# Moving two transposing chunks behind P @ V in an attention and feed-forward kernel

## The reference

```python
def reference(x, qkv_w, qkv_b, proj_w, proj_b, w_gate, w_up, w_down):
    xn = layernorm(x)                                  # x: 8 x 512 x 256
    q, k, v = split_heads(xn @ qkv_w + qkv_b)          # 16 heads of 16
    p = softmax(einsum('bnhd,bmhd->bhnm', q, k) * 0.25)
    attn = merge(einsum('bhnm,bmhd->bnhd', p, v)) @ proj_w + proj_b
    gate, up = xn @ (w_gate / 127).T, xn @ (w_up / 127).T   # hidden 768, integer weights
    ffn = (silu(gate) * up) @ (w_down / 127).T
    return x + attn + ffn
```

## Time and profile before

| | |
|---|---|
| three runs | 628.84, 630.44, 630.52 us (median 630.44) |
| profiled execution, its own time | 631.72 us |
| its span | 629.8 us, mean granted TensorE clock 0.997 |
| TensorE busy | 605.6 us (96%) |
| VectorE busy | 490.8 us (78%) |
| ScalarE busy | 373.6 us (59%) |
| GpSimd busy | 172.4 us (27%) |

### The profile page before, as it was taken

One profiled execution on the slowest core, in us unless ns is written; L12 is line 12 of the kernel. 1 busy time (PEld: TensorE's weight loads), 2 busy tenths in 40 slices (PEclk: granted clock), 3 DMA queues, 4 the chain that ended last, 5 costly groups with the idle time before them and its releaser, 6 DMA issues.

```text
span 629.8 us, 10979 instructions
## 1 busy us (share of the span) xinstructions
PE 605.6 (96%) x3616; PEld 329.5 (52%) x3616; DVE 490.8 (78%) x647; ACT 373.6 (59%) x483; POOL 172.4 (27%) x181
## 2 busy tenths in 40 slices
PE   7898999999999999999999999999999999999885
PEld 6654455554645555554545545455555455554434
DVE  5897887788887887888887887878878777878712
ACT  3545665666566565675566564766557655666571
POOL 3215144220621225220532215221252202222210
PEclk9999999999999999999999999999999999999998
DMA  8770181114612184203812166012822037221101
GB/s 277 230 120 3 68 234 52 53 36 163 157 36 50 59 245 82 51 4 130 202 50 51 34 180 162 12 50 93 230 64 51 3 124 180 51 51 36 35 2 36
DMA packets 38204, 58.98 MB, mean 94 GB/s; under 512 B 6048, under 2 KB 21280, under 8 KB 38176
## 3 DMA queue, kind: packets, MB, share of 16 engines
q1 hardware_dynamic: 38176, 58.61, 34.3%
HBM read 37.10 MB, written 20.97 MB: 92 GB/s over the span
## 4 chain that ended last, share of the span: by engine, by line
PE 85%; DVE 6%; ACT 4%; issue 3%; DMA 1%; POOL 1%; SPq 0%; ACTq 0%; DVEq 0%; POOLq 0%
PE dense L910 36%; PE o_bank L900 19%; PE st_bank L869 16%; PE s_bank L886 11%; DVE neg_max L681 3%; ACT probs L562 2%; DMA probs<-in_L_attn_qkv_w 1%; PE dense L924 1%; PE dense L941 1%; DVE o_blocks L742 1%; ACT qk_parts L578 1%; POOL xn L489 1%; PE s_bank L869 0%; PE dense L968 0%; DVE w_gl L733 0%
## 5 line engine op out<-in xcount | busy, mean ns | idle before, releaser
L562 ACT ACTIVATE probs<-st_bank 128x1024 f32<-128x1024 f32 x250 | 255.9, 1024 | 211.0 <-PE st_bank L869 206.7
L681 DVE TENSOR_REDUCE neg_max<-s_bank 128x2 f32<-128x1024 f32 x250 | 304.8, 1219 | 75.8 <-PE s_bank L886 75.0
L900 PE MATMUL o_bank<-probs,v_ones 128*32 128x512 f32 x1024 | 137.2, 608 | 3.8 <-ACT probs L562 3.8
L869 PE MATMUL st_bank<-q_stack,k_stack 50*128 50x512 f32 x500 | 124.7, 495 | 4.4 <-ACT probs L562 4.2
L497 POOL TENSOR_TENSOR hid_tl<-hid,hid_th 128x512 fp32r<-128x512 f32 x48 | 61.7, 1285 | 194.1 <-ACT hid_th L627 194.1
L886 PE MATMUL s_bank<-k_stack,q_stack 48*128 48x512 f32 x500 | 111.6, 442 | 1.2 <-DVE neg_max L681 0.2
L869 PEld LDWEIGHTS st_bank<-q_stack,k_stack 50*128 50x128 f32 x500 | 46.6, 183 | 119.7 <-ACT probs L562 82.5
L886 PEld LDWEIGHTS s_bank<-k_stack,q_stack 48*128 48x128 f32 x500 | 46.9, 184 | 28.9 <-DVE neg_max L681 26.9
L530 POOL TENSOR_TENSOR resid<-resid,p_bias 128x256 f32<-128x256 f32 x32 | 22.5, 736 | 108.9 <-DMA resid<-in_L_attn_x 108.9
L900 PEld LDWEIGHTS o_bank<-probs,v_ones 128*32 128x32 f32 x1024 | 20.2, 108 | 47.9 <-issue 42.6
L709 DVE SCALAR_TENSOR_TENSOR gated<-gated,dense 128x512 f32<-128x512 f32 x48 | 32.7, 681 | 13.2 <-ACT gated L601 11.9
(11 more groups left out here) (104 smaller groups left out, 686.3 us busy)
## 6 DMA issues: line engine op xcount, KB each, us to landing
q_spread<-qk_parts SPq DMA_DIRECT2D x16, 512.0 KB, 3.3
k_spread<-qk_parts SPq DMA_DIRECT2D x16, 512.0 KB, 3.7
q_stack<-q_spread SPq DMA_DIRECT2D x64, 128.0 KB, 3.1
k_stack<-k_spread SPq DMA_DIRECT2D x64, 128.0 KB, 3.3
q_stack<-q_spread SPq DMA_DIRECT2D x64, 64.0 KB, 3.3
k_stack<-k_spread SPq DMA_DIRECT2D x64, 64.0 KB, 3.3
resid<-in_L_attn_x SPq DMA_DIRECT2D x8, 512.0 KB, 5.3
xn<-in_L_attn_x SPq DMA_DIRECT2D x7, 512.0 KB, 3.5
```

Source lines behind the costliest of these rows:

```text
L562: nc.scalar.activation(probs[:, s % 2, 2 * half:2 * half + 2, :], transposed_bank(row, s, half)[:, :, :], ACT.Exp, scale=SCALE).then_inc(e ...
L681: nc.vector.tensor_reduce(neg_max[:, g % 2, :, NT * pair + qt], score_bank(row, half)[:, :, :], AX_X, ALU.max, negate=True).then_inc(max_d ...
L869: done = nc.tensor.matmul(transposed_bank(row, s, half)[:, r, :], k_stack[rows, pair, P * kt:P * (kt + 1)], q_stack[rows, pair, :], start= ...
L900: done = nc.tensor.matmul(o_bank[32 * j:32 * (j + 1), :], v_ones[:, kt, 8 * (g // 2) + 2 * j + g % 2, :], probs[:, (s - 1) % 2, j, :], sta ...
```

## The change

The chunk `xn` 0 goes from step 3, slot 0 to step 3, slot 1, and `xn` 1 from step 3, slot 2 to step 4, slot 1. `proj` 0 goes from step 4, slot 0 to step 3, slot 2; `proj` 1 stays. ScalarE and VectorE take `xn` 0 at step 3, slot 2 and `xn` 1 at step 4, slot 2, each ahead of the `proj` chunk that is taken there. The opening pass keeps its order: the entries of `TAKEN_AT` no longer apply to it.

```diff
-    (3, 0, "xn", 0, 1), (3, 2, "xn", 1, 1),
-    (4, 0, "proj", 0, -1), (4, 2, "proj", 1, -1),
+    (3, 1, "xn", 0, 1), (3, 2, "proj", 0, -1),
+    (4, 1, "xn", 1, 1), (4, 2, "proj", 1, -1),
...
-TAKEN_AT = {("v", 0): (0, 2)}
+TAKEN_AT = {("v", 0): (0, 2), ("xn", 0): (3, 2), ("xn", 1): (4, 2)}
...
-            return [c for c in chunks_of(row.like) if TAKEN_AT.get(c[2:4], c[:2]) == (step, slot)]
+            later = {} if row.like == -1 else TAKEN_AT
+            return [c for c in chunks_of(row.like) if later.get(c[2:4], c[:2]) == (step, slot)]
```

## The result

The changed kernel takes 650.95 us (median of 4 executions, 649.33 to 659.03) against 630.35 for the kernel before: ratio 1.0358, 95% interval 1.0268 to 1.0448. In a second comparison, 6 executions against 17, it was 652.42 against 632.73: 1.0284, 1.0227 to 1.0341. It is slower by about 20 us. The forecast was 14 us, 644.5, and its range ended at 651.0; a ratio of 1.0358 is 652.9 us on this kernel. The direction and the chain of waits came out; the size didn't, and what was missing in the sum is the granted clock.

A forecast was written before the change was run, and what follows sets the result against it. The prediction took TensorE, busy 96% of the span, as the bound. It summed 2.5 (row 0) + 5 x 2.2 (rows 1 to 5) + 0.45 (row 6) + 0.1 (row 7) to 14.0 us, forecasting 644.5 us, range 640 to 651.

The forecast's parts named there:

- The gap behind P @ V: In steps 3 and 4, P @ V itself costs TensorE 1.00 us; work put behind it costs its own length.
- st31: Matmul pair into st_bank of step 3, half 1 (digits: step, half; plain s means s_bank); forecast start 134.79.
- Rival 1: The gap behind P @ V is free after all, but the load still binds: 641.5 us; chance 0.05.
- rival 2: The gap behind P @ V is free and no one feels the load: 626.5 us; chance 0.03.
- xn 0's cover given up: Transposes leaving the real gap in step 3 lose 0.41 us of cover; 0.16 of waits is saved, 0.25 net.
- The load: Load of x issued later, landing 143.07 instead of 139.56; VectorE and TensorE wait, 2.2 us a row in rows 1 to 5.
- Rival 3: The load is hidden by an early landing or a VectorE backlog; 0.45 us a row remains: 633.6 us; chance 0.04.
- the size model: Fixed 2.0 us plus bytes at 436 GB/s: 3.2 us for 512 KB, a row loss of 1.9 instead of 2.2.
- Row 0: First row: the 1.00 us wait for POOL goes, but waits for exp and max follow; 2.5 us longer.
- Row 6 and row 7: Last two rows: transposes without a load cost 0.45 us in row 6; projection only costs 0.1 in row 7.
- the term for the clock: Granted clock expected at 1.00 in the loop, so the sum contained no time for a fall.
- rival 4: TensorE's clock falls in the new stall, six times 1.7 us, 10 us on top: 655 us; chance 0.08.

The follow-up runs named there:

- statistics-later: The changed kernel with the first statistics, and VectorE's wait for x, one step later (steps 5 to 8, not 4 to 7): 635.28 us, ratio 1.0042.
- low-part-first: The changed kernel with VectorE doing the reciprocal, low part of xn 1 and proj 1 before the wait for x and first statistics: 634.48 us, ratio 1.0062.
- the doubled load: The changed kernel with each load of x preceded by another 512 KB load into a spare tile, VectorE waiting for both: 668.95 us, ratio 1.0604.
- the filler: The changed kernel with six extra 512-column matmuls ahead of q 0 in rows 0 to 5: 645.95 us, ratio 1.0209.
- with both: The changed kernel with extra matmuls ahead of q 0 and extra identity transposes ahead of the last P @ V: 647.46 us, ratio 1.0259.

## Why the prediction was right and wrong

- **The gap behind P @ V is no gap: right.** From P @ V to the next matmul it is 1.00 us in the changed kernel too (138.88 to 139.88), and st31 came 1.59 after P @ V, where 1.41 was forecast. Rival 1 and rival 2 fell with it.
- **xn 0's cover given up, 0.25 a row up to st41, 0.45 up to proj 1: right in sum, by luck.** From st30 to proj 1 it is 7.74 us in the changed kernel (137.91 to 145.65) and was 7.29 (132.41 to 139.70): 0.45. But the wait of s41 for max40 did not come (s41 0.34 after st41), and the transposes took 0.59 instead of 0.41, twice, which I had not priced. The two errors cancelled. The price could have been read in the kernel before: in its row 0 the scores start 0.56 us after the transposes (61.17), at no wait:

```profile
61.73 0.50 PE L869 MATMUL st_bank<-q_stack,k_stack 50*128 50x512 f32 x2
```

- **The load: right.** Issue 0.85 after the transposes, landing 3.40 (3.5 assumed), VectorE's wait 1.67 (1.6), TensorE's 1.53 (1.75), 2.23 us a row (2.2). The 0.07 that I gave the semaphore stood on no row, and the 3.40 has it inside. The statistics-later and the low-part-first kernels gave the loss back, the doubled load made it grow. Rival 3, a load that is hidden, fell.
- **The landing against the size model:** by the fit of the Trainium skill ("DMA: Bandwidth & Descriptors", the anatomy of one DMA) the estimate was 3.2 us; the measured 3.3 to 3.4 lies close above it.
- **Row 0: right where the clock stayed.** With the filler st50 started at 72.02 (72.2 forecast). In the changed kernel it started at 72.44, with TensorE already at 1.2 GHz. On the way q 0 waited 1.47 us for ScalarE's copy of xn 1, which my chain for this row did not name; it ended ahead of the wait for the low part and did not move st50.
- **Row 6 and row 7:** from st30 of row 6 (515.14) to that of row 7 (588.57) 73.43 us, before 72.97 (497.08 to 570.05): 0.46, as forecast.
- **What failed is the term for the clock, which the sum put at nothing.** The prediction had "the granted clock at 1.00 in the loop", and gave a fall, rival 4, a chance of 0.08 outside the range, because "here one stall of 1.75 us stands between full steps". That is true of rows 1 to 5, where a fall behind such a stall was seen in 2 rows of 20. It is false of row 0: st40's wait for exp31 stands in the prediction's own account of that row, and the wait ahead of q 0 follows by the same chain, but I did not count them together. In the profiled execution row 1's st30 is 5.5 us later than before (137.91 against 132.41), of which 2.4 is the chain and 3.1 the clock; row 1 adds 1.3. In other executions it is more. Rival 4 itself had the cause and not the pattern: it priced six like falls of 1.7 us. I had also taken the kernel before's tail as proof of how much idleness the clock stands, from one execution of a kernel whose own clock varies from 0.983 to 1.000.

The difference between 14 and 20 us is the granted clock: at like clocks 14 us are left, 6.5 us came back with a filler, and with both the loss is 14.8. What stays open is why it falls in one execution and not in the next. The falls in rows 0 to 5 go with the stalls that the change brings. The long fall in row 7 also comes without the change, and whether the change makes it more frequent isn't shown; only the profiled executions can be looked into by stretch.

## What to carry to other kernels

When a chunk is moved that frees a buffer, follow the load that was waiting for that buffer to its first reader, and count what stands behind that reader in the same queue; here the slack was 1.9 us, the move made 1.7 us of waiting of it, and moving the reader by one step or behind the three instructions queued after it made the change cost 0.5 us a row instead of 2.2. A wait put down to an engine ahead of a weight load need not be lost time of the matmuls: look at the distance between matmul starts. And where a change brings idle stretches to a TensorE that was full, give the clock a term of its own, with a range, and count the stretches that lie close together, in the odd first row above all. When executions differ, compare them at like mean clocks.

## What the runs showed of the hardware that I had not expected

- Idle stretches of 0.97 and 1.47 us, with 3 us of work between them, were followed by ten microseconds at 1.2 GHz in one execution, by shorter falls in others, and by none in one (low part first). The same place with 1.4 us of extra matmuls kept 2.4 GHz in one profile and fell for some 3 us in another. Single stalls of 1.5 to 1.8 us were followed by a fall in 2 rows of 20, stalls of 3.2 us in 4 of 5.
- From the start of four transposes of 128 columns to the next matmul it is 0.41 us where that one uses all 128 rows (135.21 to 135.62) and 0.59 where it uses 50 (139.88 to 140.47).
- With six or twelve transposes of the identity in each of four holes of 0.9 us, the granted clock stayed at 1.00 there in four profiles of four; without them it fell in seven of ten. The Trainium skill ("TensorE: Matmul & The Clock Gate", the part on PE-mode transpose) says that transposes don't count as busy for the clock in the way that matmuls do. The counts don't bear that out for these, though ordinary matmuls stand between the holes.
